# Cross attention in float32: four head pairs per values run, and the output bank lent to two absorbing products

## What is computed

```python
def xattn(x, context, Wq, Wk, Wv, Wo, bo):        # HEADS = 16, DIM_HEAD = 64
    q, k, v = x @ Wq, context @ Wk, context @ Wv   # x: 64 x 64 x 256, context: 64 x 256 x 192
    q, k, v = heads(q), heads(k), heads(v)
    attn = softmax(einsum('bhid,bhjd->bhij', q, k) * SCALE)
    out = einsum('bhij,bhjd->bhid', attn, v)
    return out.transpose(0, 2, 1, 3).reshape(B, Nq, INNER_DIM) @ Wo + bo
x = x + xattn(layernorm(x), ctx_768, ...)
```

## Time and profile before

| | |
|---|---|
| median of 3 runs | 2362.71 (2360.82 to 2368.18) |
| profiled execution, device time | 2363.8 |
| its span | 2362.0 |
| PE busy over the span | 2217.5 (94%) |
| DVE busy | 1602.8 (68%) |
| ACT busy | 1294.7 (55%) |
| POOL busy | 844.2 (36%) |
| mean granted clock of PE | 0.974 |
| transposes L552 | x1024, 153.5 |
| values run L568 | x4096, 147.5 |

### The profile page before, as it was taken

How to read it: one execution, slowest core, us unless ns; L and a number is a source line. 1 busy time by engine, 2 the same in 40 slices (tenths; PEclk the granted TensorE clock), 3 DMA queues, 4 the chain that set the end, 5 groups by cost and what they waited for, 6 DMA issues and landing times. The chain is left out here.

```text
span 2362.0 us, 55990 instructions
## 1 busy us (share of the span) xinstructions
PE 2217.5 (94%) x18992; PEld 1996.2 (85%) x18992; DVE 1602.8 (68%) x3655; ACT 1294.7 (55%) x3906; POOL 844.2 (36%) x1022
## 2 busy tenths in 40 slices
PE   6999999999999999999995999999999966999996
PEld 5889888998889888998895999999999853888885
DVE  6666666766666666766655889898888856444442
ACT  4555555555555555555544666667666621444442
POOL 3333333333333333333332222222222222677664
PEclk9999999999999999999997999999999986999998
DMA  4000000000000000000004000000000011444334
GB/s 114 19 20 27 9 27 18 27 9 27 27 18 27 9 27 18 27 9 27 13 6 152 1 20 9 18 18 9 18 9 18 14 43 45 103 79 105 77 53 104
DMA packets 61946, 82.52 MB, mean 35 GB/s; under 512 B 9936, under 2 KB 45520, under 8 KB 61808
## 3 DMA queue, kind: packets, MB, share of 16 engines
q1 hardware_dynamic: 48912, 63.46, 8.5%
q0 software_dynamic: 12960, 18.12, 4.6%
HBM read 59.80 MB, written 25.96 MB: 36 GB/s over the span
## 5 line engine op out<-in xcount | busy, mean ns | idle before, releaser
L411 POOL TENSOR_TENSOR p_sb<-p_sb,rinv 128x512 f32<-128x512 f32 x256 | 279.2, 1090 | 809.3 <-DVE rinv L757 809.3
L669 ACT ACTIVATE p_sb<-s_ps,nmax 128x256 f32<-128x256 f32 x512 | 238.3, 470 | 186.5 <-DVE nmax L735 183.3
L735 DVE TENSOR_REDUCE nmax<-s_ps 128x2 f32<-128x512 f32 x256 | 176.8, 691 | 224.4 <-PE s_ps L65 220.3
L915 POOL TENSOR_TENSOR sp_sb<-sp_sb,srinv 128x512 f32<-128x512 f32 x128 | 133.3, 1041 | 426.1 <-DVE srinv L1109 426.1
L45 ACT CAST qk_hi<-qk_ps 128x512 fp32r<-128x512 f32 x248 | 147.0, 593 | 130.1 <-PE qk_ps L65 128.8
L1057 ACT ACTIVATE sp_sb<-sm_sb,snmax 128x128 f32<-128x128 f32 x512 | 199.3, 390 | 7.1 <-DVE snmax L1120 4.0
L754 DVE COPY pt_sb<-t_ps 128x512 f32<-128x512 f32 x256 | 176.8, 691 | 21.3 <-PE t_ps L552 7.4
L46 ACT ACTIVATE q_sb<-m_ps 64x256 fp32r<-64x256 f32 x256 | 96.9, 379 | 171.8 <-PE m_ps L65 168.0
L65 PE MATMUL qk_ps<-q_sb,wkt_hi 128*128 128x256 f32 x496 | 147.7, 320 | 26.1 <-DVE qk_hi L57 16.6
L552 PE MATMUL t_ps<-ident,p_sb 128*128 128x128 f32 x1024 | 153.5, 272 | 1.0 <-DVE pt_sb L754 1.0
L552 PEld LDWEIGHTS t_ps<-ident,p_sb 128*128 128x128 f32 x1024 | 126.5, 141 | 29.1 <-issue 1.2
(11 more groups left out here) (293 smaller groups left out, 7587.5 us busy)
## 6 DMA issues: line engine op xcount, KB each, us to landing
ctx_raw<-in_ctx_t SPq DMA_DIRECT2D x32, 256.0 KB, 2.8
ctx_raw<-in_ctx_t SPq DMA_DIRECT2D x64, 128.0 KB, 3.0
x_ring<-in_x SPq DMA_DIRECT2D x16, 256.0 KB, 2.8
x_mid<-x_ring SPq DMA_DIRECT2D x16, 256.0 KB, 2.2
xn<-f_xn SPq DMA_DIRECT2D x16, 256.0 KB, 2.2
acc<-x_sb SPq DMA_DIRECT2D x16, 256.0 KB, 2.3
e_raw<-in_gate SPq DMA_DIRECT2D x8, 512.0 KB, 3.9
e_raw<-in_up SPq DMA_DIRECT2D x8, 512.0 KB, 5.0
```

The lines of the kernel that those rows point to most:

```text
L411: nc.gpsimd.tensor_tensor(prob, prob, inv, ALU.mult).then_inc(norm_done, 1)
L669: ex = nc.scalar.activation(p_sb[:, k, b * J:(b + 1) * J], s_ps[1 - w][:, b * J:(b + 1) * J], ACT.Exp, bias=nmax[:, k, b:b + 1], scale=1.0 ...
L735: nc.vector.tensor_reduce(nmax[:, (p - 1) % 4, :], s_ps[1 - w][:].rearrange("p (b j) -> p b j", b=2), AX_X, ALU.max, negate=True).then_inc ...
L915: nc.gpsimd.tensor_tensor(prob, prob, inv, ALU.mult).then_inc(norm_done, 1)
```

## The change

The values run moves to steps 3 and 7 and takes four head pairs in a row, 32 matmuls of the program, filling the whole bank `o_ps`. `ot_hi` and `ot_lo` become one instruction of 128 x 512 each in those steps. `pt_sb` gets a fifth slot, with a table of slots. The early absorbing product goes into `o_ps`, which is free between step 7 and step 3, and the table puts early units in steps 1 and 2 of the odd tile instead of 1 and 3.

```diff
-            pt_sb = sbuf(ph, "pt_sb", [P, 4, HALF])
+            pt_sb = sbuf(ph, "pt_sb", [P, 5, HALF])
...
-            ODD_UNIT = {(1, False): 0, (1, True): 1, (2, True): 2, (3, False): 3, (3, True): 4,
+            ODD_UNIT = {(1, False): 0, (1, True): 1, (2, False): 2, (2, True): 3, (3, True): 4,
...
+            PT_SLOT = (3, 0, 1, 2, 4, 0, 1, 2)
...
-                    bank = y_ps if two_banks and h else qk_ps
+                def absorb(m, pair, h, two_banks, mid=False, after_mid=False):
+
+                    bank = o_ps if mid else y_ps if two_banks and h else qk_ps
                     wait(pe, q_done, m + 1)
-                    wait(pe, qk_done, 2 * m + h - (1 if two_banks else 0))
+                    wait(pe, qk_done, 2 * m + h - (1 if two_banks or mid or after_mid else 0))
...
                         if early is not None and not first:
-                            absorb(*early[:3], two_banks=False)
+                            if p == 1:
+                                pe.wait_ge(ot_done, 2 * t - 1)
+                            absorb(*early[:3], two_banks=False, mid=True)
...
-                        if w == 1 and (not first if p < LAG_PV else cur):
+                        if p % 4 == 3 and (not first if p < LAG_PV else cur):
 
                             pe.wait_ge(t_done, n - 3)
                             pe.wait_ge(v_done, PAIRS * t + (4 if p >= LAG_PV else 0))
-                            wait(pe, ot_done, PAIRS // 2 * t + (p - 5) // 2 - 1)
-                            if first and p == LAG_PV + 1:
-                                pe.wait_ge(wk_done, PAIRS)
-                            for q in ((p - 5) % PAIRS, (p - 4) % PAIRS):
+                            wait(pe, ot_done, 2 * t - (1 if p < LAG_PV else 0))
+                            if u == 1 and look and p < LAG_PV:
+                                pe.wait_ge(qk_done, 2 * PAIRS * (t // 2 + 1) + 3)
+                            for q in range((p + 1) % PAIRS, (p + 1) % PAIRS + 4):
...
-                            mm.then_inc(pv_mm, 2)
+                            mm.then_inc(pv_mm, 4)
...
                         if late is not None and not first:
-                            absorb(*late[:3], two_banks=False)
+                            absorb(*late[:3], two_banks=False, after_mid=early is not None)
...
-                        if w == 1 and (not first if p < LAG_PV else cur):
+                        if p % 4 == 3 and (not first if p < LAG_PV else cur):
                             act.wait_ge(pv_mm, n - 3)
                             if p >= LAG_PV:
                                 wait(act, y_mm, t)
-                            split_hi_act(nc, ot_part(ot_hi, (p - 4) % PAIRS), o_half(p)).then_inc(ot_hi_done, 1)
+                            split_hi_act(nc, ot_part(ot_hi, p), o_ps[:]).then_inc(ot_hi_done, 1)
...
                             dve.wait_ge(t_mm, n - 2)
-                            wait(dve, pv_mm, n - 6)
-                            nc.vector.tensor_copy(pt_sb[:, (p - 3) % 4, :], t_ps[:]).then_inc(t_done, 1)
+                            wait(dve, pv_mm, PAIRS * t - (0 if p >= LAG_PV else 4))
+                            if first and p == LAG_T:
+                                weights.wait_split(dve, O_SPLIT)
+                            nc.vector.tensor_copy(pt_sb[:, PT_SLOT[(p - 3) % PAIRS], :], t_ps[:]).then_inc(t_done, 1)
```

More of the change, by code:

```diff
@@ L451, in project_q @@
                                                             xt_hi[:, d, :], xt_lo[:, d, :])]).then_inc(q_mm, 1)
-                def absorb(m, pair, h, two_banks):
-                    bank = y_ps if two_banks and h else qk_ps
+                def absorb(m, pair, h, two_banks, mid=False, after_mid=False):
+                    bank = o_ps if mid else y_ps if two_banks and h else qk_ps
                     wait(pe, q_done, m + 1)
-                    wait(pe, qk_done, 2 * m + h - (1 if two_banks else 0))
+                    wait(pe, qk_done, 2 * m + h - (1 if two_banks or mid or after_mid else 0))
                     for c in range(2):
@@ L565, in tile @@
                                         k = 2 * b + j
-                                        c = (4 * ((p - 5) // 2 % 2) + 2 * (q % 2) + b) * HEAD
+                                        c = (2 * (q % 4) + b) * HEAD
                                         for h in range(2):
@@ L569, in tile @@
                                                            v_sb[:, k, q * P + h * HEAD:q * P + (h + 1) * HEAD],
-                                                           pt_sb[:, q % 4, k * P + h * HEAD:k * P + (h + 1) * HEAD],
+                                                           pt_sb[:, PT_SLOT[q], k * P + h * HEAD:k * P + (h + 1) * HEAD],
                                                            start=(j == 0), stop=(j == 1))
-                            mm.then_inc(pv_mm, 2)
+                            mm.then_inc(pv_mm, 4)
                         if p == 4 and not first:
@@ L576, in tile @@
                                 weights.wait_split(pe, O_SPLIT)
-                            pe.wait_ge(ot_done, PAIRS // 2 * t)
+                            pe.wait_ge(ot_done, 2 * t)
                             wait(pe, y_added, t - 1)
@@ L603, in four, with ot_part @@
                 return a.rearrange("p (t q) -> p t q", t=4)
[L605 to L611, removed]
+            def ot_part(ot, p):
+                return ot[:, (p + 1) % PAIRS:(p + 1) % PAIRS + 4, :].rearrange("p a t -> p (a t)")
             def wkt_part(wkt, pair):
@@ L623, in q_hi, with absorbed_hi @@
                         split_hi_act(nc, q_sb[r, pair % 2, h, :], m_ps[r, 0:2 * P], SCALE).then_inc(q_hi_done, 1)
-                def absorbed_hi(m, pair, h, used, two_banks):
-                    bank = y_ps if two_banks and h else qk_ps
+                def absorbed_hi(m, pair, h, used, two_banks, mid=False):
+                    bank = o_ps if mid else y_ps if two_banks and h else qk_ps
                     act.wait_ge(qk_mm, 2 * m + h + 1)
@@ L680, in tile @@
                         if early is not None and not first:
-                            absorbed_hi(*early, two_banks=False)
+                            absorbed_hi(*early, two_banks=False, mid=True)
                         if p == PAIRS - 1 and u == 0 and look:
                             xt_hi_copy(t // 2 + 1)
-                        if w == 1 and (not first if p < LAG_PV else cur):
+                        if p % 4 == 3 and (not first if p < LAG_PV else cur):
                             act.wait_ge(pv_mm, n - 3)
@@ L706, in q_lo, with absorbed_lo @@
                     lo.then_inc(q_done, 1)
-                def absorbed_lo(m, pair, h, two_banks):
-                    bank = y_ps if two_banks and h else qk_ps
+                def absorbed_lo(m, pair, h, two_banks, mid=False):
+                    bank = o_ps if mid else y_ps if two_banks and h else qk_ps
                     dve.wait_ge(qk_hi_done, 2 * m + h + 1)
@@ L745, in tile @@
                         if early is not None and not first:
-                            absorbed_lo(*early[:3], two_banks=False)
+                            absorbed_lo(*early[:3], two_banks=False, mid=True)
                         if first and 1 <= p < 3:
@@ L757, in tile @@
                             nc.vector.reciprocal(rinv[:, (p - 1) % 4, :], rsum[:, (p - 1) % 4, :]).then_inc(rinv_done, 1)
[L758 to L761, removed]
+                        if p % 4 == 3 and (not first if p < LAG_PV else cur):
+                            dve.wait_ge(ot_hi_done, 2 * t + (1 if p >= LAG_PV else 0))
+                            split_lo_dve(nc, ot_part(ot_lo, p), o_ps[:], ot_part(ot_hi, p)).then_inc(ot_done, 1)
                         if p == 5 and not first:
```

## The result

The changed kernel takes 2338.28 (median of 4 runs, 2334.42 to 2340.26), the kernel before beside it 2363.03 (2360.82 to 2368.18): a ratio of 0.989 with a 95% interval of 0.987 to 0.9911. The forecast was 2338.2. The profiled execution has a span of 2336.3 against 2362.0.

What follows compares the result with a forecast made beforehand. PE was taken as the bound. A group gains 1.48 + 1.28 - 1.05 = 1.71, times 15 = 25.7; with + 0.45 + 0.64 - 0.93 - 1.37 that is 24.5, from 2362.7 to 2338.2, range 2330 to 2351.

Steps and rivals of the forecast that it cites:

- Waits removed: Odd tile, steps 1 and 3: three PE waits for the emptying of `qk_ps` go, 1.48 a group.
- The merge: Values runs joined in pairs: each of four merges a group saves 0.32, together 1.28.
- The rival in which the switch is paid by the pass: Merging runs saves nothing; a group gains 0.43, time 2357; chance 0.03.
- New waits: Uncovered late units wait for DVE's split: 0.65 in even step 1, 0.20 in each step 5; 1.05 a group.
- Moved at no cost: Odd tile: the early unit moves from step 3 to step 2, counted 0, upper bound 0.4 a group.
- The last group: Last even tile: without statistics, its step 1 waits 0.20 and not 0.65, adding 0.45 to the gain.
- The ends: Outside the groups: tile 0 costs 0.93, tile 31's two merges gain 0.64, the drain costs 1.37.
- the term put at nothing: Tile 0, step 5: the values run taken out was counted as no gain, within 0 to 1.25.
- the sum of the drain: Drain: 0.93 for the longer last run plus 0.44 for the later splits, 1.37 against.
- the fourth rival: Groups: longer blocks of transposes and values run lower PE's clock, 1.7 a fall, time about 2447; chance 0.04.
- The clock rival: The fourth rival: a 2.54 block of transposes and values run makes PE look idle, 1.7 a fall; chance 0.04.

Runs made afterwards that it cites:

- e3: The changed kernel with DVE splitting the late unit ahead of the maximum of the scores in every step: 2333.49, ratio 0.988.
- e7_best: The changed kernel with DVE's split ahead of the maximum except in step 2 of the odd tile, and two values runs in the drain: 2320.25.
- e2_bank_only: The kernel before, four values runs a tile kept, with only the early units of steps 1 and 3 moved to the final product's bank: 2340.81.
- e4: The changed kernel with the layer norm's statistics moved on DVE from step 0 to 1 of the even tile, POOL's power from 1 to 2: 2334.02.

## Why the prediction was right

**Waits removed.** 1.48 a group forecast; all three are gone in the trace of after, and by itself the bank gave 1.55. The 0.07 more goes with the early unit of step 3, whose block took 0.58 behind its wait and takes 0.48 without; the sum had left that out.

**The merge.** 0.32 each from a run cut in the middle; the long run took 2.01 as worked out. A step with it takes 5.49 where one with the short run took 4.54, so 0.95 more and not 0.93: each merge saved 0.30. The rival in which the switch is paid by the pass is out. The Trainium skill's floor of about 25 ns between starts ("TensorE: Matmul & The Clock Gate", "Wait — 56ns, not 53.3ns?") would have made it 0.45 and the time 2330; the 32 passes more took 2.08 - 1.15 = 0.93, again 29 ns each, which the floor allows, so the rows were the better price.

**New waits.** 0.65 in step 1 of the even tile, 0.66 measured; 0.20 in each step 5, as in step 6 before. Their cause was confirmed twice, by the order of DVE (a group of 74.48 to 73.46, of which 0.2 is the old wait of step 6) and by the statistics alone (74.48 to 74.00).

**Moved at no cost.** Step 3 of the odd tile didn't wait for DVE's copy: its transposes start at 609.62, the copy of step 2 ends at 608.77 + 0.69:

```profile
608.77 0.69 DVE L754 COPY pt_sb<-t_ps 128x512 f32<-128x512 f32 x1
```

0.16 were left. That "it fits, with little to spare" was right, and e3 shows what 0.8 more costs there: a wait of 0.7, and 0.89 on the step.

**The last group.** For the groups and the last even tile 26.1 were forecast, and 25.69 measured: the last group gained 2.04, 0.35 more than the others, where 0.45 was added, and fourteen gained 1.69.

**The ends** were wrong, in both directions, and the errors largely cancelled: the start came out 3.45 better than forecast, the end 1.94 worse. That the total came so near is luck. The start was forecast 0.93 longer and came out 2.52 shorter. Steps 1 to 3 of tile 0, from scores to scores, take 19.84 before and 17.65 after. These are the windows of before, of after and of e7_best, which has the changed tile 0:

```profile
31.36:51.20 19.84, 17.11 (x102) 15.58 (x100) 14.32 (x28) 13.16 (x31) 2.08 (x2) 0.83 0.19 54
...
31.47:49.12 17.65, 14.92 (x100) 13.38 (x100) 14.32 (x28) 13.06 (x31) 2.09 (x2) 1.00 0.23 59
...
30.95:50.56 19.61, 17.10 (x101) 15.54 (x100) 14.19 (x28) 13.16 (x31) 2.08 (x2) 0.83 0.18 54
```

The changed tile 0 has both times, by the clock, and so has that of before: e2_bank_only takes 17.91 at 1.00. These 2.19 are no part of the change, and tile 1 begins anywhere between 70.95 and 74.85 in the seven other traces with the changed tile 0. The later steps are the change. Steps 4 to 6 took 17.29 before and 15.92 after; all eight traces with the changed tile 0 read 15.9 to 16.1, the two with the old one 17.3. Of these 1.37, 0.82 is step 5, from which the run was taken and for which I had counted nothing, within 0 to 1.25; why step 4 gave another 0.42 stays open. Step 7 took 8.23 instead of 7.30, the 0.93 forecast. So the change made the start 0.44 shorter, where the sum had it 0.93 longer: the term put at nothing was the wrong one.

At the other end a net of 0.73 was forecast, 1.37 for the drain less 0.64 for tile 31's merges, and it was 2.67. Tile 31 gave 0.60. The drain, from its first scores to the last addition, took 16.18 instead of 12.91, so 3.27 more. From the start of the last run to the final product 3.45 was forecast and 5.09 measured, and the difference is the run, 3.68 at a granted clock of 0.50 instead of 2.08; the final product took 0.28 more, and had mostly been at the low clock before as well. In the trace of e3_split_first, whose drain is the same program at a clock of 1.00, run to final product is 1225.30 - 1221.81 = 3.49. So the run's own length and its rounding were priced rightly, and the term that failed is the clock, which the sum of the drain didn't have. That is the mechanism of the fourth rival. I had priced it for the groups, where it didn't happen, and left it out of the drain, the one place where the earlier trace rows already showed it. Its scatter is large: from one addition to the last, the same drain took 19.5 in the trace of e3, 20.9 in that of e4 and 23.0 in the changed kernel's, so a good part of the 2.67 is luck.

**The clock rival** was wrong about its cause. A block of transposes and values run of 2.54 leaves the clock alone, 60 times in the groups (1.00 from 73.27 to 1189.89). A wait of 1.8 right behind transposes was followed by a fall 12 times in 15, and with the wait filled there was none. The Trainium skill's same page, section "Part 4: PE-mode transpose", says that transposes don't count as busy the same way; the runs don't show it. They show that idling behind transposes was punished and the same stretch with ordinary matmuls in it was not, which would fit idling alone as well. No run here tried idling of that length without transposes.

## What to carry to other kernels

Two edits of one change need not add. Here the second bank was worth 1.55 a group by itself and the merge on top of it 0.14. Joining small matmuls into one run saves a run's entry and exit, 0.3 each here, but takes away the cover under which another engine empties a bank, and pays only once the next product has another bank to go to. Where PE is the bound, look for what the shortest step no longer hides, and take the price from a step that is short already. And an edit that helps before another may hurt after it: moving the statistics was worth 0.48 a group while DVE's split waited behind them, and cost 0.4 once it didn't. The best of the kernels tried, 2320.25, has the change, the split ahead of the maximum in all steps but one, and two runs in the drain.

## What the hardware showed that I had not expected

The clock fall has a price that the wait does not show. In the merge-only kernel PE waited 2.0 in step 1 of the odd tile, where the kernel before had waited 0.78; the clock took another 1.5 in 12 of 15 groups, and the fall came after the wait, while PE was busy again (0.72 over the next 6.0). The profile's row of waits counts none of it, since the matmuls are only further apart. Twelve matmuls for nothing in each group made the kernel 20 faster, 18 of it in the groups.
